# The lambdas image by image in four parts, the last value blocks' low parts in spare memory, and edits around the joint queries

## The reference, cut to what matters

```python
# x: (32, 128, 32, 32), normalised in 32 groups of channels; n = m = 1024 positions, d = 128
keys    = xf @ Wk.T                              # b, m, 16
softmax_keys = softmax(keys, axis=1)
values  = bn(xf @ Wv.T, gamma_v, beta_v)         # b, m, 32
queries = bn((xf @ Wq.T)...)                     # b, 16, n, 4
content_lambda   = einsum('bmk,bmv->bkv', softmax_keys, values)
position_lambdas = einsum('nmk,bmv->bnkv', E, values)     # nearly all of the work
out = x + einsum('bknh,bkv->bhvn', queries, content_lambda) \
        + einsum('bknh,bnkv->bhvn', queries, position_lambdas)
```

## Time and profile before

| | |
|---|---|
| median of 3 runs | 1443.67 us (1443.24 to 1444.08) |
| the profiled execution | 1445.38 us, span 1443.3 us |
| PE busy | 1422.0 us, 99% of the span, 14608 matmuls |
| DVE, ACT, POOL busy | 818.6, 727.5, 434.0 us |
| mean granted PE clock | 0.997 |

### The profile page before, as it was taken

The page is one execution under the profiler, slowest core; times in us unless marked ns, Lnnn a source line. Parts: engine busy times, 40 slices in busy tenths (PEclk is TensorE's granted clock), DMA queues, the critical chain, the costliest instruction groups (busy, mean ns, idle before and its releaser), DMA issues.

```text
span 1443.3 us, 36541 instructions
## 1 busy us (share of the span) xinstructions
PE 1422.0 (99%) x14608; PEld 1192.6 (83%) x14608; DVE 818.6 (57%) x1258; ACT 727.5 (50%) x1109; POOL 434.0 (30%) x366
## 2 busy tenths in 40 slices
PE   8999989999999999999999999999999999999998
PEld 7997878888888888888888888888888888888876
DVE  8989555555555555555555555555555555555543
ACT  6775545545444455545444455545444455445442
POOL 6683122322233222322233222322233222322230
PEclk9999999999999999999999999999999999999999
DMA  9835243442344333443344333442344333443331
GB/s 308 290 126 105 49 90 61 93 94 67 79 94 94 80 78 76 93 91 69 80 94 94 80 77 77 93 92 68 80 94 94 80 76 78 93 92 68 80 89 16
DMA packets 475810, 134.77 MB, mean 93 GB/s; under 512 B 339984, under 2 KB 471168, under 8 KB 475264
## 3 DMA queue, kind: packets, MB, share of 16 engines
q1 hardware_dynamic: 475776, 134.32, 39.2%
HBM read 109.12 MB, written 25.17 MB: 93 GB/s over the span
## 4 chain that ended last, share of the span: by engine, by line
PE 95%; DVE 2%; issue 1%; ACT 1%; DMA 1%; POOL 0%; DVEq 0%; ACTq 0%; POOLq 0%
PE ps_a L1262 80%; PE ps_b L1274 5%; PE ps_a L1246 4%; PE ps_b L1141 3%; PE ps_a L1131 1%; DVE bn L731 1%; PE ps_b L1200 1%; DMA e_nat<-in_L_conv_E 0%; ACT q_diag L669 0%; DMA x_main<-in_x 0%; DVE q_stats L756 0%; DVE v_stats L750 0%; ACT e_hi L587 0%; DVE key_diag L794 0%; POOL v_rstd L469 0%
## 5 line engine op out<-in xcount | busy, mean ns | idle before, releaser
L1262 PE MATMUL ps_a<-v_hi,e_hi 128*128 128x512 f32 x1708 | 668.8, 392 | 0.0
L1262 PE MATMUL ps_a<-v_hi,e_lo 128*128 128x512 f32 x1708 | 665.5, 390 | 0.1
L669 ACT ACTIVATE q_diag<-q_blk,q_shift_n,q_scale_n 128x256 f32<-128x256 f32 x512 | 410.2, 866 | 124.5 <-PE ps_b L1274 124.5
L587 ACT ACTIVATE e_hi<-e_nat 128x512 fp32r<-128x512 f32 x305 | 193.7, 636 | 473.6 <-PE ps_a L1262 203.7
L1262 PE MATMUL ps_a<-b_lo,e_hi 128*128 128x512 f32 x976 | 379.6, 389 | 0.0
L1262 PEld LDWEIGHTS ps_a<-v_hi,e_hi 128*128 128x128 f32 x1708 | 321.1, 188 | 67.2
L1262 PEld LDWEIGHTS ps_a<-v_hi,e_lo 128*128 128x128 f32 x1708 | 321.2, 188 | 66.3 <-issue 0.6
L497 POOL TENSOR_TENSOR e_nat<-e_nat,s_buf 128x512 f32<-128x512 f32 x61 | 97.9, 1605 | 644.4 <-DVE e_lo L761 644.4
L1262 PE MATMUL ps_a<-t_lo,e_hi 128*128 128x512 f32 x732 | 285.7, 390 | 0.0
L761 DVE TENSOR_TENSOR e_lo<-e_nat,e_hi 128x512 fp32r<-128x512 f32 x305 | 220.7, 740 | 44.7 <-ACT e_hi L587 44.7
L1262 PEld LDWEIGHTS ps_a<-b_lo,e_hi 128*128 128x128 f32 x976 | 183.2, 188 | 38.1
(11 more groups left out here) (135 smaller groups left out, 983.7 us busy)
## 6 DMA issues: line engine op xcount, KB each, us to landing
e_nat<-in_L_conv_E SPq DMA_DIRECT2D x128, 512.0 KB, 3.8
res<-in_x SPq DMA_DIRECT2D x128, 128.0 KB, 3.8
out_dram<-res SPq DMA_DIRECT2D x124, 128.0 KB, 2.6
x_main<-in_x SPq DMA_DIRECT2D x24, 512.0 KB, 5.9
q_dram<-q_nat SPq DMA_DIRECT2D x4, 2048.0 KB, 8.3
q_blk<-q_dram SPq DMA_DIRECT2D x32, 256.0 KB, 3.0
x_more<-in_x SPq DMA_DIRECT2D x8, 512.0 KB, 8.6
out_dram<-res SPq DMA_DIRECT2D x4, 64.0 KB, 2.7
```

What stands on the lines that cost most here:

```text
L587: nc.scalar.activation(e_hi[:, i], e_source(i), ACT.Copy).then_inc(e_hi_ready, 1)
L669: ins = nc.scalar.activation(to[:, n], of, ACT.Identity, bias=q_shift_n[:, n:n + 1], scale=q_scale_n[:, n:n + 1])
L1262: ins = nc.tensor.matmul(BANK_OF[odd][i], e[:, i, j].rearrange("p n k -> p (n k)"), v[:, j], start=(STARTS[odd][i] and j == 0 and n == 0), ...
```

## The change

1. `lambda_half` becomes `lambda_part`: four parts of two `j` each, one behind each of the plain sums j = 4, 5, 6, 7 of pair 0. A product now takes one image (16 rows of keys by 32 columns of values), on one of four groups of the array's columns; there are 256 of them where there were 64. `sum_lambdas` goes image by image too (32 products, before 4). `lam_scale` needs no mask: four reciprocals and four multiplications of 16 rows.
2. The key maxima's steps on PE stand one plain sum later.
3. The low parts of values 4 and 6 for pair 0 (and value 4 for pair 1) are written into memory that `res` (`first_b21_lo`) and `pos` (`first_b22_lo`) use later, so they need not wait for `t_raw`. The real `value_split_lo(6)` and `value_split_lo(4)` come later on DVE, and PE waits for them before the second half of pair 1 and of pair 2. The loads of `res` must wait until pair 1 is finished, and the loads of `E` for pair 2 go ahead of them.
4. `normalise(7)` moves from ACT to DVE, and ACT writes `v_hi` for j = 4 ahead of `normalise(3)` and `(2)`.
5. `query(0)` moves from the end of pair 1 into pair 2.
6. DVE writes the last evacuation of pair 3 ahead of its last split for pair 4, and writes out one block of four pairs more ahead of its loop.
7. SP waits before its loop until the first joint queries are done.
8. In the last joint queries one block product stands between the two halves (`apart`).

```diff
-            sp.wait_ge(lam_summed, 1)
+            next_e(1)
+            sp.wait_ge(first_summed, 8)
             load_res(0, 0)
             load_res(1, 1)
-            next_e(1)
             next_e(2)
...
             odd_loads(3, 1, 1)
+            sp.wait_ge(queried, PPB)
             with sp.Fori(1, BLOCKS - 1) as blk:
...
             def lam_scale():
                 dve.wait_ge(lam_summed, 1)
-                link(nc.vector.reciprocal(inv_sum[:], sum_ps))
...
+                for a in range(A):
+                    rows = slice(a * V, a * V + KD)
+                    ins = nc.vector.reciprocal(inv_sum[rows], sum_ps[rows])
                 link(ins)
                 dve.wait_ge(lam_zeroed, 1)
...
+                for a in range(A):
+                    rows = slice(a * V, a * V + KD)
+                    nc.vector.tensor_tensor(lam_diag[rows].rearrange("p (g a v) -> p a g v", a=A, v=V)[:, a],
+                                            lam_ps[rows].rearrange("p (g v) -> p g v", v=V),
+                                            inv_sum[rows].unsqueeze(2).to_broadcast([KD, G, V]), ALU.mult
+                                            ).then_inc(lam_masked, G // A)
...
+            def lambda_part(part):
+                if part == 0:
                     pe.wait_ge(keys_exp, A)
+                    pe.wait_ge(v_normed, 2)
+                else:
+                    pe.wait_ge(v_normed_act, (0, 2, 4, 5)[part])
+                if part == A - 1:
+                    pe.wait_ge(v_normed, 3)
+                for j in (2 * part, 2 * part + 1):
+                    for g in range(G):
+                        for a in range(A):
+                            ins = nc.tensor.matmul(lam_ps[a * V:a * V + KD, g * V:(g + 1) * V], keys[:, j, g, a],
+                                                   v_nat[:, j, (g * A + a) * V:(g * A + a + 1) * V],
+                                                   start=(j == 0 and g == 0), stop=(j == J - 1), skip_group_check=True)
+                ins.then_inc(lam_part, 1)
...
+                    elif j >= MJ and p < 2 - col:
+                        lo = (first_b21_lo, first_b22_lo)[col][:, j % MJ]
...
-                if j == 0:
+                if j == 1:
                     turn_key_max(A - 1, B)
-                if j == 1:
+                if j == 2:
                     spread_key_top(A - 1)
-            lambda_half(0)
-            pe.wait_ge(e_lo_ready, NP)
-            for j in range(MJ, J):
-                pe.wait_ge(v_hi_ready, j + 1)
-                plain_sums(0, j, (0, 1))
-                if j == MJ + 1:
-                    lambda_half(1)
+                if j >= MJ:
+                    lambda_part(j - MJ)
             sum_lambdas()
...
+                    if p == 2 and j == 0:
+                        query(0, first=True)
                 ins.then_inc(half_done, 1)
                 pe.wait_ge(e_lo_ready, p * NP + NP)
+                pe.wait_ge(v_lo_ready, (0, 5, 6)[p])
...
                 query_images(0, 0)
+                if apart:
+                    product(p + 2, 0, 1)
                 query_images(1, 1).then_inc(queried, 2)
...
             product(PAIRS - 2, 0, 0)
-            query_group(PAIRS - 4)
-            for i in range(1, NP):
+            query_group(PAIRS - 4, apart=True)
+            for i in range(2, NP):
```

More of the change, by code:

```diff
@@ L146, in lambda_conv_kernel @@
         early.close()
+        early = ExitStack()
+        first_b21_lo = sb("first_b21_lo", [P, MJ, BC], f32r, stack=early)
+        early.close()
         res = sb("res", [P, G * NH, 2, GN])
@@ L644, in _ @@
             values_hi(3)
+            act.wait_ge(q_stored[1], 16)
+            act.wait_ge(q_stats_done, 2)
+            values_hi(4)
             normalise(3)
@@ L653, in _ @@
                 normalise(j - 1)
-            normalise(J - 1)
             for n in range(4):
@@ L1044, in _ @@
             query_affine()
+            nc.vector.tensor_tensor(t_raw[:, 2], raw_block(v_nat, 1, 0), t_raw[:, 1], ALU.subtract).then_inc(t_ready, 1)
+            dve.wait_ge(t_ready, 4)
+            value_split_lo(4)
+            first_lo(2, 3)
+            evacuate_first(1)
             t_split_lo(1, 1)
             t_split_lo(2, 2)
-            first_lo(2, 3)
-            evacuate_first(1)
             add_out(0)
@@ L1060, in _, with pair @@
             evacuate_u2(PLAIN, 1)
-            def pair(p, i, last=False):
+            def pair(p, i, first=False, last=False):
                 odd = i % 2
-                evacuate_c12(p - 1, 1 - odd)
+                if not first:
+                    evacuate_c12(p - 1, 1 - odd)
                 split_lo(p, 6)
@@ L1094, in _ @@
             evacuate_c21(PLAIN, 1)
-            for n in range(3, NP - 1):
+            for n in range(3, NP - 2):
                 split_lo(PPB, n)
-            with dve.Fori(1, BLOCKS - 1) as blk:
+            evacuate_c12(PLAIN, 1)
+            split_lo(PPB, NP - 2)
+            for i in range(PPB):
+                pair(PPB + i, i, first=(i == 0))
+            with dve.Fori(2, BLOCKS - 1) as blk:
                 for i in range(PPB):
@@ L1301, in _ @@
             pe.wait_ge(e_lo_ready, 2)
-            for j in range(MJ):
+            for j in range(J):
                 if j == 0:
@@ L1341, in plain_pair @@
                     plain_sums(p, j, (0, 1, 2))
-                if p == 1:
-                    query(0, first=True)
+                    if p == 1 and j == MJ:
+                        average_queries()
                 plain_sums(p, J - 1, (0, 1, 2), last=True)
```

93 lines of the change are left out of this document (39 added, 54 removed).

## The result

The changed kernel takes 1439.01 us (median of nine runs, 1437.55 to 1440.25) against 1443.67 for the kernel before: a ratio of 0.9968, 95% interval 0.9959 to 0.9977. The forecast was 1440.5 in 1436.3 to 1443.3.

A forecast was written before the change was run, and what follows sets the result against it. PE, busy 99% of the span, was taken to bound the kernel by its work and idle stretches. Terms 0.2 + 0.8 + 1.0 + 1.2 = 3.2 us less took the median from 1443.67 to 1440.5, range 1436.3 to 1443.3.

The forecast's parts named there:

- Lambdas and sums, the matmuls alone: Pair 0 on PE: four bursts of 1.15 us and sums of 0.6 replace 8.1 us; 2.5 us less.
- Instructions: Lambda bursts two to four wait 0.4, 0.5, 0.5 us for instruction blocks, the sums 2.4; 3.8 us more.
- DVE behind the sums: Before pair 1: DVE needs 9.7 us to the first evacuation, PE's own way 9.4; PE waits 0.3 us.
- First stretch together: Plain sums' start to pair 1: the terms 1.6 + 2.5 - 3.8 - 0.3 give 0.0; 0.2 us less kept for overlaps.
- Pairs 1 and 2: Same work, DVE's later low parts covered by PE's matmuls (by 0.8 us, then by a hair); zero change.
- Evacuation: Ahead of the first joint queries: DVE evacuates one split earlier, so PE's wait goes; 0.8 us less.
- First joint queries: A block takes 3.6 us, not 4.6, as E's loads wait: 2.4 us idle where 3.4 were; 1.0 us less.
- Last joint queries: Block product between the halves leaves a wait of 0 to 0.9 us where 1.5 + 0.1 were; 1.2 us less.
- The clock: Granted clock falls once behind PE's idles, as before: zero change, with 2.5 us either way.
- rival (b): Clock holds through both 2.4 us idles, behind the lambdas and in the first joint queries: 2.5 us less, 1438.0; chance 0.19.
- Rival (c): Instruction blocks arrive in time in the lambdas: 3.8 us less, 1436.7; chance 0.15.
- Rival (e): Blocks take 4.6 us in the lambdas too, waits grow and the clock falls again: 1447.0 us; chance 0.06.

The follow-up runs named there:

- the run with 144 fillers: Changed kernel plus 144 do-nothing instructions (already satisfied semaphore waits of PE) in pairs 1 and 2: 1441.65 us, ratio 0.9987 to the kernel before.
- the second profile: The changed kernel measured once more, unaltered, on another chip: 1439.70 us, ratio 0.9969 to the kernel before.
- the pair of kernels with the same ends: Kernel before with 112 do-nothing instructions, 1449.26 us; the same plus SP's wait, DVE's order with unrolled evacuation, and the values apart, 1441.78 us.

## Why the prediction was right, and where it was not

The time came out 1.5 us under the forecast. The first stretch was 1.2 worse than its term, the first joint queries with their second wait 0.9 better, the last ones 0.3 better; that the errors nearly cancel is luck. The two profiled spans differ by 6.0 us, and the stretches give it as: start 0.4 less, first stretch 0.95 more, pairs 1 and 2 0.1 more, pair 3 0.7 less, first joint queries 2.5 less, the pass behind them 1.3 less, the loop 0.2 more, last joint queries 1.5 less, from query(30) to the end 0.8 less. The first and the last of these were not in the sum: in the runs with the change's start the first plain sum came anywhere from 104.8 to 106.7 us, and why the end is shorter no run shows.

- **Lambdas and sums, the matmuls alone** (2.5 less): a burst is 1.2 us by the rows (1.15 forecast) and the sums some 0.7. PE's busy time in the stretch fell by 1.8 us with the waits left out, so somewhat less than 2.5.
- **Instructions** (3.8 more): 0.54, 0.37 and 0.19 for 0.4, 0.5 and 0.5, and 2.23 for 2.4; 3.3 in all. Places and mechanism were right. The short ones are not steady: with the same ends in the bursts, the run with 144 fillers had none of 0.4 us or more there, only the wait in the sums. That one, in six profiled executions with the same lambdas and ends, was 2.23, 2.24, 2.24, 2.51, 2.79 and 2.79 us.
- **Key maxima** (1.6 less): the wait is gone.
- **DVE behind the sums** (0.3 more): 1.08. This is the term that was mis-sized in the first stretch; the scaling is 2.75 us, inside my 1.5 to 3 and above the 2.1 that I took. From there to the end of the first evacuation DVE needs 10.3 us for the 9.7 of the sum, and the difference is the scaling.
- **First stretch together**: 0.2 less was forecast, 0.95 more came, 1.25 in the second profile. I had also kept 0.2 "for overlaps" that nothing shows.
- **Pairs 1 and 2** (zero): 0.1 more, without a wait for DVE. The cover held.
- **Evacuation** (0.8 less): 0.7 in the trace (pair 3 to the queries, 21.85 us for 22.58). Undoing it cost 2.2, since the fetch hangs on it too.
- **First joint queries** (1.0 less): 2.5, and 0.6 of it came back as a second wait in the product behind. The step that failed is "3.6 - 1.2 = 2.4 us of idle". It starts the fetch with the queries; PE's queue enters the block earlier, once it is not held at the semaphore for `pos`. The evacuation and the fetch are one term, not two. The second wait stands where the next end falls, 16 instructions behind the queries; the sum has no term for it.
- **Last joint queries** (1.2 less): 1.5. Their wait is 0.22 us on the weight loads, in the 0 to 0.9 expected.
- **The clock** (zero, 2.5 either way): in the first profile it held through both idles, as rival (b) has it, and gave 1.3 us of the pair behind. Over the runs it is a draw: mean 0.9980 and 0.9987, for 0.998 before. The forecast "falls once, as before" was right in what it gives, and a single profile would have misled. Behind the wait in the sums it held at 2.23 and at one of the 2.24 us, and fell at the other 2.24, at 2.51 and at both of 2.79 us. A wait of 2.71 us in pair 1's query() left it at 1.00, 2.99 us in the same place did not. Between 2 and 2.8 us the rows don't decide; behind all of 2.99 us and more it fell.

Rival (c), no waits in the lambdas, fell with the first trace. It is what the Trainium skill's Runtime: NRT & Kernel Launch, Instruction fetch mechanics, would give, as the prediction said. That section also says that a taken branch out of the two pages at hand forces a fetch. The trace does not show this for PE's loop (875 instructions by my count, over three blocks): no packet of instructions starts during its passes. Rival (e), slower, came nowhere near. That the gain is nothing but an accident of the ends falls by the pair of kernels with the same ends, 7.2 us for the later half, and by the 1.9 us that are left with 144 fillers. But how large the gain is does hang on them: 2.0 us of it by the medians, 2.6 by the ratios, went with 144 fillers.

What stays open: why the waits in the bursts and in the sums differ between executions with the same ends, why the clock falls behind one idle of 2.24 us and not behind another, and the parts of the medians that no trace shows (1.0 us without SP's wait, 1.5 with the values not apart).

## What to carry to other kernels

Where an engine runs hundreds of small instructions in a row, count its instructions in the program and mark the block ends: a wait stood wherever all or nearly all 256 between two ends were small, of 0.8 to 1.9 us where the queue could come early to the front end and of 2.0 to 3.8 us where it could not. One long operation among them (a block product of 2.7 us here) took it down to 0.2 us. Any edit that adds or removes instructions ahead moves all later ends, so compare versions with equal ends, by fillers few enough to hide, before the difference is given to the edit; and look at every run of small instructions in the program, not only at the ones that you edit. Products four times as wide were as fast in all as four times as many narrow ones, since the matmul time that the narrow form saved came back as fetch waits and as more operations for the engine behind.

## What the runs showed of the hardware that I had not expected

- 112 instructions that do nothing made a program of 5,626 instructions 5.9 us slower, 0.4%, by their place alone.
- Semaphore waits that are long satisfied are free for PE only up to a number: eight behind two split matmuls were hidden (9.86 us for 9.78 in the stretch), 14 were not (16.20, 0.32 us more for each of 20 banks).
- An operation late by 0.34 us lengthened a fetch wait by 1.0 us (by 0.75 against the longest wait seen without it): the instruction packet started 0.9 us behind the first query and not with it, the queue having been held at the semaphore.
- The same idle of 2.2 us was followed by half the clock in one execution and by the full clock in another, of the same program; over six executions of the same lambdas the clock fell in four.
